# Attention's turned one-hots: one VectorE comparison in place of two ScalarE activations

## The reference, cut to what matters

```python
q = einsum('ni,hid->nhd', x, Wq) + bq      # k and v alike
e = edge_attr[:, None, None] * We[None]
ke = k[src] + e
alpha = einsum('ehd,ehd->eh', q[dst], ke) / sqrt(d)
m = segment_max(alpha, dst)
ex = exp(alpha - m[dst])
w = ex / segment_sum(ex, dst)[dst]
agg = segment_sum(w[:, :, None] * (v[src] + e), dst)
```

## Time and profile before

| | us |
|---|---|
| median of 2 runs | 6225.09 |
| lowest and highest | 6212.45 and 6237.72 |
| the profiled execution, its time | 6235.4 |
| the profiled execution, its span | 6233.7 |

### The profile page before, as it was taken

One profiled execution on the slowest core, in us unless ns is written; L12 is line 12 of the kernel. 1 busy time (PEld: TensorE's weight loads), 2 busy tenths in 40 slices (PEclk: granted clock), 3 DMA queues, 4 the chain that ended last, 5 costly groups with the idle time before them and its releaser, 6 DMA issues. The chain is left out here.

```text
span 6233.7 us, 93450 instructions
## 1 busy us (share of the span) xinstructions
PE 3934.2 (63%) x20652; PEld 3207.9 (51%) x20652; DVE 3660.7 (59%) x11663; ACT 2829.9 (45%) x6936; POOL 4383.7 (70%) x4477
## 2 busy tenths in 40 slices
PE   5667766675676666668888875334433356665655
PEld 4566666664555555546566554333333356664443
DVE  6788888876888888767777763111111044445555
ACT  3788888871111111256555653111111178782333
POOL 2676776655777777757777775777777777777664
PEclk8787788877888888878888886555555589997777
DMA  4444444444555555632222224223222255551113
GB/s 123 126 130 125 129 129 125 127 94 139 164 138 135 135 140 134 134 62 75 74 74 74 74 74 82 74 77 77 76 75 76 59 157 164 162 160 55 50 50 39
DMA packets 485366, 649.31 MB, mean 104 GB/s; under 512 B 120187, under 2 KB 332938, under 8 KB 484822
## 3 DMA queue, kind: packets, MB, share of 16 engines
q0 software_dynamic: 155552, 345.75, 21.7%
q1 hardware_dynamic: 329271, 297.58, 17.5%
HBM read 495.44 MB, written 150.71 MB: 104 GB/s over the span
## 5 line engine op out<-in xcount | busy, mean ns | idle before, releaser
L693 POOL DMA_INDIRECT e_ring<-table,gather_i x880 | 926.2, 1052 | 287.2 <-issue 266.2
L693 POOL DMA_INDIRECT kv_ring<-keys_values,gather_i x880 | 860.3, 978 | 380.1 <-issue 245.8
L2132 POOL DMA_INDIRECT rows_by_src<-rs_out,key x880 | 869.8, 988 | 320.9 <-issue 262.6
L693 POOL DMA_INDIRECT gl_ring_f<-table,gather_i x880 | 854.8, 971 | 340.2 <-issue 250.1
L693 POOL DMA_INDIRECT e_ring<-filter_rows,gather_i x880 | 840.4, 955 | 304.4 <-issue 267.9
L2102 PE MATMUL rs_ph<-nodes,rs_hot_t 128*128 x1760 | 450.2, 437 | 684.7 <-ACT rs_out L2119 661.1
L2102 PEld LDWEIGHTS rs_ph<-nodes,rs_hot_t 128*128 128x128 f32 x1760 | 388.0, 325 | 747.3 <-issue 747.1
L2063 DVE TENSOR_SCALAR rs_hot_t<-rs_rows,part 128x512 f32<-128x512 bf16 x220 | 116.1, 529 | 983.1 <-PE rs_ph L2102 967.2
L2271 PE MATMUL gl_sum_f<-gl_ring_f,gl_hot_f 128*128 128x128 f32 x1760 | 301.1, 325 | 473.8 <-DVE arena L2318 261.3
L1547 PE MATMUL e_pa<-e_msg,e_hot 128*128 128x128 f32 x3520 | 564.5, 313 | 32.8 <-DVE e_msg L1741 25.5
L742 DVE TENSOR_TENSOR arena<-arena,e_pa 128x128 f32 x1760 | 496.5, 282 | 124.9 <-PE e_pa L1547 82.5
(11 more groups left out here) (458 smaller groups left out, 9835.5 us busy)
## 6 DMA issues: line engine op xcount, KB each, us to landing
rows_by_src<-e_filler SPq DMA_DIRECT2D x256, 260.0 KB
arena<-rows_by_src SPq DMA_DIRECT2D x256, 260.0 KB
at_rows<-local_rows SPq DMA_DIRECT2D x220, 128.0 KB, 3.5
e_rows<-local_rows SPq DMA_DIRECT2D x220, 128.0 KB
rs_rows<-local_rows SPq DMA_DIRECT2D x220, 128.0 KB
e_attr<-edge_attr SPq DMA_DIRECT2D x880, 25.0 KB
kv_ring<-keys_values,gather_i POOLq DMA_INDIRECT x880
e_ring<-table,gather_i POOLq DMA_INDIRECT x880
```

The costliest lines, as they stand in the source:

```text
L693: pool.indirect_dma_start(ring[:, r, u, :], None, table, bass.IndirectOffsetOnAxis(index, 0)).then_inc(arrived[r], 16)
L2132: pool.indirect_dma_start(table, bass.IndirectOffsetOnAxis(place, 0), out[:, r, u, :], None, bounds_check=SLOTS_R - 1, oob_is_err=False).t ...
```

## The change

The two activations go from ScalarE's queue. VectorE gets one `tensor_scalar` with `is_equal` for each batch, bf16 in and float32 out, at the head of its slot: behind the loads of bucket numbers and ahead of the scans and the products. It waits for the same two things: the rows of its batch, and the query that last read its half of `hot_t`. `hots_t` now counts one for each batch in place of two, on SyncE and TensorE too.

```diff
@@ sync
-                at_least(sp, hots_t, 2 * (k - R + 1), None)
+                at_least(sp, hots_t, k - R + 1, None)
@@ tensor, query(k)
-                at_least(pe, hots_t, 2 * (k + 1), None)
+                at_least(pe, hots_t, k + 1, None)
@@ scalar
-            def turned_hot(k):
-                q, r = k % 2, k % R
-                to = hot_t[:, q, :, :].rearrange("p u f -> p (u f)")
-                act.wait_ge(rows_in[r], 16 * (k // R + 1))
-                at_least(act, queried, k - 1, None)
-                act.activation(to, rows[:, r, :], ACT.Abs, bias=c.part[:, 0:1], scale=-1.0).then_inc(hots_t, 1)
-                act.wait_ge(hots_t, 2 * k + 1)
-                act.activation(to, to, ACT.Relu, bias=c.ones[:, 0:1], scale=-1.0).then_inc(hots_t, 1)
...
-                if s == 0:
-                    turned_hot(0)
                 if 0 <= s - LAG < BATCHES:
                     edge_hot(s - LAG)
-                if s + 1 < BATCHES:
-                    turned_hot(s + 1)
                 if 0 <= s - 1 < BATCHES:
                     keep_values(s - 1)
@@ vector
+            def turned_hot(k):
+                q, r = k % 2, k % R
+                dve.wait_ge(rows_in[r], 16 * (k // R + 1))
+                at_least(dve, queried, k - 1, None)
+                dve.tensor_scalar(hot_t[:, q, :, :].rearrange("p u f -> p (u f)"), rows[:, r, :], c.part[:, 0:1], None, ALU.is_equal).then_inc(hots_t, 1)
...
                 which = loaded_values(nc, c.bucket_d, ka, DVE_ENGINE, NT - 1) if adding else None
+                if s == 0:
+                    turned_hot(0)
+                if s + 1 < BATCHES:
+                    turned_hot(s + 1)
                 if chain and ph == 2:
                     scan_runs(n)
```

## The result

| | before | after |
|---|---|---|
| median, us | 6225.09 (2 runs) | 6301.65 (2 runs) |
| lowest and highest | 6212.45 and 6237.72 | 6301.27 and 6302.02 |
| the profiled execution's span | 6233.7 | 6299.6 |

The ratio is 1.012, with a 95% interval of 1.0083 to 1.0157: slower by 1.2%, less than the 2% that the prediction counts as no change. Predicted were 6273 us and a range of 6205 to 6345. Beside the experiments the kernel before was measured again, with medians of 6224.7, 6228.8 and 6228.1 us over 12 or 13 runs each, so its 6225 stands.

The account below looks back on a forecast made before the run. VectorE, with TensorE in answer to it, was taken to pace attention, while ScalarE had slack. The terms 88 + 5 + 3 - 37 - 11 = +48 us on 6225.1 us gave 6273 us, range 6205 to 6345.

Parts of the forecast that it names:

- VectorE's part: In attention, 220 added comparisons at 0.40 us of queue time cost 88 us, plus 5 us for slower ones.
- Cover: In attention, 37 us of the comparisons would fall into waits VectorE has anyway, mostly for TensorE and gathers.
- ScalarE's credit: In attention, a quarter of the 43.3 us TensorE waited for ScalarE would be gained: 11 us.
- Rows land long before they are needed: At the comparison, SyncE's ring four deep and buffers freed in the same slot as before: no cost.
- The wait for `query`: At the comparison, waiting for the query two batches earlier was costed at nothing, bounded by 13.0 us.
- The start: At attention's start, first one-hot and query come behind VectorE's memset: about 3 us more, bounds 0 and 5.
- the likeliest case: Whole kernel: the forecast itself, 6273 us, spanning 6245 to 6300 us, chance 0.61.
- The faster one: In attention, ScalarE's slack reaches VectorE and all 109 us of its waits vanish: -18 us, 6207 us, chance 0.18.
- ScalarE as the bound: In attention, ScalarE set the pace after all, so the stage falls to the gathers' pace: 6126 us, chance 0.03.
- No cover at all: In attention, every wait shifts with the comparison: +119 us, 6344 us, chance 0.12.
- The held comparison: In attention, a comparison is held until a running gather ends: 76 us in all, 6349 us, chance 0.06.
- What the profile was to show: Signs in attention: comparison means of 480 to 530 ns, VectorE over 87% busy, ScalarE about 56%, changed waits.

Follow-up runs that it names:

- e4: Kernel before without ScalarE's two steps and with no VectorE comparison after batches 0 and 1, so outputs are wrong: 6226.8 us, ratio 1.0002.
- e5: Kernel before with the load of pen three steps later, plus the same comparison on VectorE into an unread tile, ScalarE's steps kept: 6281.4 us, ratio 1.0086.
- e10: Kernel before with the load of pen later and VectorE's head_sums over half of the features: 6196.3 us, ratio 0.9948.
- e1: Changed kernel with the load of pen three steps later in SyncE's queue: 6277.2 us, ratio 1.008 to the kernel before.
- e7: Changed kernel with pen load later; VectorE compares only in slots of phases 2 and 3, ScalarE makes the other half: 6248.9 us, ratio 1.0034.
- e8: Changed kernel with pen load later; VectorE compares only in slots of phases 0 and 1, ScalarE makes the other half: 6243.8 us, ratio 1.0027.
- e11: Kernel before with pen load later and VectorE's weigh step made by ScalarE in four small activations a batch: 6267.5 us, ratio 1.0062.

## Why the prediction was right or wrong

**What bounds the kernel: right.** VectorE with TensorE in answer to it, not ScalarE, was read from who waits for whom at equal busy time. e4, e5 and e10 show it directly.

**VectorE's part, 88 + 5 us: right, with 7 us too much.** It measured 85.9 us of busy time, 0.39 us each. The start-to-start reading of the earlier trace rows was the right unit, since the durations themselves add to 110.1 us; the 5 us for slower ones did not come. For ScalarE I added durations up, 314 us, where its busy time fell by 283.

**Cover, 37 us: right in size, wrong in its picture.** The waits on TensorE and gathers shrank by 113.6 - 76.7 = 37 us, and in e1, without late rows, by 113.6 - 70.6 = 43 us. But I had counted slots that hold a wait, at full cover each, and no cover elsewhere. e7 and e8 say that it isn't so: moving the comparisons to the slots with waits gave nothing. Slack that is shared along a chain of slots, and used up little by little, would fit these two runs and the table; that is my reading, and no run isolates it. So the 37 us are right partly by luck.

**ScalarE's credit, 11 us: wrong, it is 0.** e4 gives 1.0002, which leaves room for 4 us at most, and e5 stands beside e1. Of the 43.3 us in which TensorE waited for ScalarE, the 23.6 at `total` became waits for VectorE's messages in e4, and the 19.7 at L916 stayed.

**"Rows land long before they are needed": wrong, and this is the step that failed.** It counted the depth of the ring (four batches) and the point at which a buffer is free, and not what stands in SyncE's queue between: a load of `pen` that waits for `scan_all` one slot ahead of the rows' use. It had been costed at nothing, and is worth 24 us by e1, most of the 28.6 us by which 6273 us was too low. To name the queues that a step is moved past was part of the work; I named SyncE's and looked at one of its two waits only.

**The wait for `query`, bounded at 13.0 us: right.** It is 3.7 us, and 6.3 in e1. **The start, 3 us: right.** The first product comes 3.8 us later than before (176.35 against 172.55 us), of which 0.5 us were there ahead of the memset.

**The sum.** 86 (comparisons) - 37 (cover) + 30 (rows and query) - 9 (mostly VectorE's own register loads, whose idle times fell from 77 to 69 us) = 70 us in attention of the profiled pair, and 76.6 us by the medians, against the forecast 48. 6301.65 us is inside the range, just outside the 6245 to 6300 of the likeliest case. Without the late rows it is e1's 50 us by its ratio, next to the forecast's 48, and that closeness is luck. Counted as above, e1's profile has 86 (comparisons) - 43 (cover) + 6 (`query`) - 2 (VectorE's own register loads) = 47 us. The 11 us of ScalarE's credit that didn't come, and the waits for `query`, were made up by a cover 6 us larger than forecast and by the 7 us that VectorE's part had too much.

**The rivals.** The faster one (all waits vanish) and ScalarE as the bound are excluded by e4. No cover at all is excluded by the 37 us, and by e1's 50 us for 86 us of work. The held comparison is excluded by its durations: with GpSimd busy as before, the mean is 501 ns and the longest 736. From 200 to 1360 us of the changed kernel, 137 comparisons began while a gather ran, with a median of 486 ns and a mean of 506; 62 began with none, with 485 and 489. So the Trainium skill's rule in "SBUF — State Buffer", section "Who interferes with whom", that the second of the two engines to issue blocks fully, isn't borne out for VectorE as the second. The rule is for modes of VectorE that use both ports, and no trace names the mode in which the comparison ran. For GpSimd as the second it is in part: of 72 gathers that began during a comparison in that stretch 16 took over 1150 ns (up to 1554), but the median is 950 ns, as without one. The mean of all 880 went from 978 to 994 ns, 14 us in all, which lay in GpSimd's slack.

**What the profile was to show.** ScalarE at 56% (577 us of 1000 measured), waiting for VectorE and TensorE: as said. TensorE naming ScalarE hardly at all: only in part, 24.6 us are left (16.3 at L916, 8.3 at `total`). VectorE over 87%: 86.4%. Waits on TensorE from 98 to 50 us: 70. The last comparison at 1415 us: 1429.9, and 1406.5 without late rows. GpSimd's wait on L1013 was to shrink: it grew from 99.0 to 109.4 us, and the one on the products from 28.1 to 65.6. Together that is 47.9 us more. GpSimd's own work hardly changed while attention got 69 us longer, so it had to wait longer for whoever frees the ring.

## What to carry to other kernels

Between two engines of equal busy time, ask whom the others wait for. Here work taken from the one that was seldom waited for was worth nothing, though it was busy 84% of the time, and work put on the other cost four to seven tenths of itself. When a consumer moves to an earlier point, read the queue of who feeds it, entry by entry: a buffer that is free doesn't help while its load stands behind an entry that waits for something else. A cheap step on the wrong engine can be dearer than two steps on the one with slack.

## What was not expected

ScalarE's relief is worth nothing (e4, 283 us taken away, 0.02%), yet a burden on it costs: e11 put (1186 - 1026) / 220 = 0.73 us a batch on it, by its busy time in attention, and lost 42 us. That fits a kernel that stands near the corner where both engines would bind, but as e11 also makes part of each message later, it isn't shown. The stretch of attention in e11:

```profile
158.00:1480.00 1322.00, 886.13 (x4972) 796.74 (x4972) 1028.37 (x3237) 1186.03 (x3680) 842.31 (x866) 0.78 0.43 117
```

Small activations are dear: 128x8 elements in 291 ns, where 128x128 took 387 ns in the kernel before (L1004); both read a scale or a bias from memory.
